# Twisted recurrence two steps at a time on GpSimd, with coefficients from VectorE and the eigenvector operations spread over the last attention halves

## What is computed

```
h = max(layernorm(x), 0);  x = x + L0(h, adj, ...)   # two graph convolutions, then LSTMs over windows of 1 to 4
h = max(layernorm(x), 0);  x = x + L1(h, adj, W, a)  # graph attention
h = max(layernorm(x), 0);  x = x + L2(h, adj, ...)   # causal attention
h = max(layernorm(x), 0);  x = x + L3(h, adj, ...)   # spectral mixer
# L3:
deg = sum(A, 0) + sum(A, 1) - diagonal(A)
L_norm = d_inv_sqrt[:, None] * (diag(deg) - A) * d_inv_sqrt[None, :]
_, U = eigh(L_norm)
out = relu((U.T @ features) @ W1 + b1) @ W2 + b2
return U @ out
```

## Time and profile before

| | us |
|---|---|
| median of 3 runs | 1045.47 |
| the 3 runs | 1045.47, 1047.27, 1044.97 |
| the profiled execution's own time | 1047.09 |
| its span (first to last instruction) | 1045.4 |
| PE busy | 873.1 |
| DVE busy | 761.5 |
| ACT busy | 493.2 |
| POOL busy | 229.3 |

### The profile page before, as it was taken

How to read it: one execution, slowest core, us unless ns; L and a number is a source line. 1 busy time by engine, 2 the same in 40 slices (tenths; PEclk the granted TensorE clock), 3 DMA queues, 4 the chain that set the end, 5 groups by cost and what they waited for, 6 DMA issues and landing times.

```text
span 1045.4 us, 14893 instructions
## 1 busy us (share of the span) xinstructions
PE 873.1 (84%) x4310; PEld 600.8 (57%) x4310; DVE 761.5 (73%) x3137; ACT 493.2 (47%) x1079; POOL 229.3 (22%) x732
## 2 busy tenths in 40 slices
PE   4689989999998999999999964999653699990598
PEld 3578865555555766766555553677442376760465
DVE  6877778887777688877777787799799696443433
ACT  0047865553434344344333310788542577860475
POOL 2111111111111111121121100121224135886000
PEclk9999999999999799999999975999976799995699
DMA  7000000000000000000000000000000000000022
GB/s 272 1 1 1 1 1 0 1 1 1 1 0 1 1 1 1 1 1 1 0 1 1 1 1 0 1 1 2 0 1 0 1 1 1 2 2 0 20 61 81
DMA packets 13976, 12.24 MB, mean 12 GB/s; under 512 B 1092, under 2 KB 10823, under 8 KB 13895
## 3 DMA queue, kind: packets, MB, share of 16 engines
q1 hardware_dynamic: 10704, 8.46, 2.5%
q10 hardware_dynamic: 3190, 2.84, 0.9%
HBM read 7.10 MB, written 4.19 MB: 11 GB/s over the span
## 4 chain that ended last, share of the span: by engine, by line
issue 49%; PE 17%; POOL 17%; DVE 15%; ACT 2%; POOLq 0%; DVEq 0%; ACTq 0%
PE bank L547 16%; POOL col_root L349 8%; POOL t L396 2%; DVE tt L785 2%; POOL PP L396 2%; DVE stat L793 2%; POOL u L396 2%; POOL XI L353 2%; DVE HT L785 1%; PE bank L557 1%; DVE X L785 1%; DVE uu L785 1%; DVE X L786 1%; POOL m L396 1%; ACT T L440 1%
## 5 line engine op out<-in xcount | busy, mean ns | idle before, releaser
L484 ACT ACTIVATE G<-bank,bias 128x512 f32<-128x512 f32 (+1 forms) x252 | 159.9, 635 | 251.7 <-PE bank L547 250.9
L547 PE MATMUL bank<-HT,wih 128*128 128x512 f32 (+1 forms) x504 | 250.6, 584 | 0.5 <-ACT HT L470 0.5
L349 POOL TENSOR_TENSOR col_root<-sa,neg_half 128x1 f32<-128x1 f32 x126 | 79.5, 631 | 491.4 <-DVE sa L787 491.4
L547 PE MATMUL bank<-H,whh 128*128 128x512 f32 (+1 forms) x288 | 136.3, 555 | 0.0
L440 ACT ACTIVATE T<-X,nbias,rstd 128x128 f32<-128x128 f32 x256 | 104.7, 487 | 39.5 <-DVE nbias L786 39.5
L444 ACT COPY T<-bank 128x512 f32<-128x512 f32 x128 | 75.0, 586 | 78.7 <-PE bank L547 50.4
L547 PEld LDWEIGHTS bank<-ST 128*128 128x128 f32 x254 | 47.9, 203 | 72.1 <-DVE ST L785 43.8
L547 PEld LDWEIGHTS bank<-HT,wih 128*128 128x128 f32 x504 | 81.0, 195 | 10.8 <-issue 4.6
L557 PE MATMUL bank<-ident,T 128*128 128x128 f32 x256 | 41.4, 287 | 43.5 <-ACT T L504 21.9
L547 PEld LDWEIGHTS bank<-XI,A 128*128 128x128 f32 x252 | 46.8, 202 | 48.8 <-DVE A L786 32.8
L547 PE MATMUL bank<-ident,ST 128*128 128x127 f32 (+62 forms) x252 | 57.5, 311 | 18.8 <-DVE ST L787 17.8
(11 more groups left out here) (331 smaller groups left out, 1855.1 us busy)
## 6 DMA issues: line engine op xcount, KB each, us to landing
out_x<-T SPq DMA_DIRECT2D x16, 256.0 KB, 2.3
wih<-in_WihT ACTq DMA_DIRECT2D x1, 1024.0 KB
whh<-in_WhhT ACTq DMA_DIRECT2D x1, 1024.0 KB
qkvT<-in_WqkvT ACTq DMA_DIRECT2D x1, 192.0 KB
wg<-in_Wg ACTq DMA_DIRECT2D x2, 64.0 KB
l3w<-in_L3W ACTq DMA_DIRECT2D x2, 64.0 KB
adjT<-in_adjT ACTq DMA_DIRECT2D x1, 64.0 KB
adj<-in_adj SPq DMA_DIRECT2D x1, 64.0 KB, 2.0
```

The costliest lines, as they stand in the source:

```text
L349: e.tensor_tensor(out=col["root"][:, :], in0=sa[:, 0:1], in1=neg_half[:, :], op=ALU.pow).then_inc(root_ready, 1)
L484: e.activation(G[x.h][:, gate, 0:n], gate_bank(k)[:, 0:n], ACT.Tanh if gate == 2 else ACT.Sigmoid, bias=bias[:, 4 * (x.p - 1) + gate:4 * ( ...
L547: mm = lambda out, l, r, start=True, stop=True: e.matmul(out, l, r, start=start, stop=stop)
```

## The change

Four parts.

1. The recurrence takes two steps at a time. From `p(s)` and `p(s-1)` both next values come as `CA * p(s) + CB * p(s-1)`, where `CA = (D0, D1*D0 + N1)` and `CB = (N0, D1*N0)` for the pair's coefficients. An operation then handles 4 elements in a partition instead of 2, and a pair of steps takes three of them (`u2`, `t2`, add). The rescaling is as before.
2. DVE computes `CA` and `CB`, in the space of the LSTM weights `wih`, behind `DLP` and `N2P`; `tw_in` is now raised four times. `N2P`'s second copy is waited for.
3. The matmul that broadcasts `lam` moves from the end of PE's attention into it, after slot 27 (`LAMBDA_AFTER`, causal attention with k = 7), and goes to bank 7.
4. The operations on the vectors are cut into parts 0 to 5. With `VECTORS` = 4, part 0 stands after half 67, part 1 after half 68, part 2 after half 69, part 3 after half 70 (`stats_1`), then `stats_2(4)`, then parts 4 and 5. The operations and their order among themselves are the same.

```diff
+VECTORS = 4
+LAMBDA_AFTER = slot_of_block(len(POINTS) * NB - 1) + 3
...
+        pair = lambda a: a.rearrange("p (s k c) -> p s k c", k=2, c=2)
+        lstm_weights = wih[:, :, :, :].rearrange("p s g o -> p (s g o)")
+        CA, CB = pair(lstm_weights[:, 0:2 * P]), pair(lstm_weights[:, 2 * P:4 * P])
...
-            e.wait_ge(tw_in, 2)
+            e.wait_ge(tw_in, 4)
             for g in range(P // KB):
-                twist(TP(u2[0][:, :], PP[:, g, 0, :], N2P[:, g * KB, :], ALU.mult))
-                for j in range(KB):
-                    s = g * KB + j
-                    k = twist.note(TP(t2[:, :], PP[:, g, j + 1, :], DLP[:, s, :], ALU.mult))
-                    if j < KB - 1:
-                        twist.note(TP(u2[(j + 1) % 2][:, :], PP[:, g, j + 1, :], N2P[:, s + 1, :], ALU.mult))
-                    e.wait_ge(ch_p, k)
-                    if s < P - 1:
-                        twist(TP(PP[:, g, j + 2, :], t2[:, :], u2[j % 2][:, :], ALU.add))
+                for j in range(0, KB, 2):
+                    n = (g * KB + j) // 2
+                    two = lambda k: PP[:, g, k, :].unsqueeze(1).to_broadcast([P, 2, 2])
+                    twist.note(TP(u2[:, :, :], two(j), CB[:, n], ALU.mult))
+                    twist(TP(t2[:, :, :], two(j + 1), CA[:, n], ALU.mult))
+                    if n < P // 2 - 1:
+                        twist(TP(PP[:, g, j + 2:j + 4, :], t2[:, :, :], u2[:, :, :], ALU.add))
...
+                if j == LAMBDA_AFTER:
+                    e.wait_ge(lam_rdy, 1)
+                    mm(bank[7][:, 0:P], bc(col["lam"][:, 0:1]), ident[:, :]).then_inc(lam_ps, 1)
...
-            e.wait_ge(lam_rdy, 1)
-            mm(bank[6][:, 0:P], bc(col["lam"][:, 0:1]), ident[:, :]).then_inc(lam_ps, 1)
...
-            e.tensor_copy(out=N2P[:, :, 0], in_=ne2p[:, 0:P]).then_inc(tw_in, 1)
-            e.tensor_copy(out=N2P[:, :, 1], in_=ne2p[:, 1:P + 1][:, ::-1]).then_inc(tw_in, 1)
+            link.note(e.tensor_copy(out=N2P[:, :, 0], in_=ne2p[:, 0:P]))
+            link(e.tensor_copy(out=N2P[:, :, 1], in_=ne2p[:, 1:P + 1][:, ::-1]))
+            by_two = lambda t: t[:, :, :].rearrange("p (s k) c -> p s k c", k=2)
+            D0, D1, N0, N1 = by_two(DLP)[:, :, 0], by_two(DLP)[:, :, 1], by_two(N2P)[:, :, 0], by_two(N2P)[:, :, 1]
+            k = link.note(TT(CA[:, :, 1], D1, D0, ALU.mult))
+            TT(CB[:, :, 1], D1, N0, ALU.mult).then_inc(tw_in, 1)
+            e.tensor_copy(out=CB[:, :, 0], in_=N0).then_inc(tw_in, 1)
+            e.tensor_copy(out=CA[:, :, 0], in_=D0).then_inc(tw_in, 1)
+            e.wait_ge(ch_e, k)
+            TT(CA[:, :, 1], CA[:, :, 1], N1, ALU.add).then_inc(tw_in, 1)
...
             while halves < N_HALVES:
                 attentions(halves)
+                vectors(halves - (N_HALVES - VECTORS))
                 halves += 1
-            e.wait_ge(tw_done, 1)
...
             stats_2(4)
...
+            for part in range(VECTORS, 6):
+                vectors(part)
```

More of the change, by code:

```diff
@@ new lines, in _, with vectors @@
+            by_half, diff2, choice, diff1 = msk[:, 16:18], msk[:, 18:20], msk[:, 20:21], msk[:, 21:22]
+            def vectors(part):
+                if part == 0:
+                    e.wait_ge(tw_done, 1)
+                    link(TS(PP[:, :, :, :], PP[:, :, :, :], 1e-26, None, ALU.add))
+                    link(e.reciprocal(out=RP[:, :, :, :], in_=PP[:, :, 1:KB + 2, :]))
+                if part == 1:
+                    link.note(TT(by_block(QQ), PP[:, :, 2:KB + 2, :], RP[:, :, 0:KB, :], ALU.mult))
+                    link(TT(by_block(RQ), PP[:, :, 1:KB + 1, :], RP[:, :, 1:KB + 1, :], ALU.mult))
+                    link(TT(gq[:, :], QQ[:, :, 0], QQ[:, ::-1, 1], ALU.add))
+                    link(TT(gq[:, :], gq[:, :], DLP[:, :, 0], ALU.subtract))
+                    link(TT(gq[:, :], gq[:, :], gq[:, :], ALU.mult))
+                    link(e.tensor_reduce(out=c("mn"), in_=gq[:, :], axis=AX.X, op=ALU.min))
+                    link(TS(msk[:, :], gq[:, :], c("mn"), None, ALU.is_le))
+                    link(STT(msk[:, :], msk[:, :], -1000.0, iota_f[:, :], ALU.mult, ALU.add))
+                    link(e.tensor_reduce(out=c("idx"), in_=msk[:, :], axis=AX.X, op=ALU.min))
+                    link(TS(c("idx"), c("idx"), 1000.0, None, ALU.add))
+                    link(TS(oneh[:, :], iota_f[:, :], c("idx"), None, ALU.is_equal))
+                if part == 2:
+                    link(TT(aB[:, :], eneg[:, 0:P], RQ[:, ::-1, 1], ALU.mult))
+                    link(TT(aF[:, :], eneg[:, 1:P + 1], RQ[:, :, 0], ALU.mult))
+                    link(e.tensor_tensor_scan(zb[:, :], aB[:, :], oneh[:, :], 0.0, ALU.mult, ALU.add))
+                    link(e.tensor_tensor_scan(zf[:, ::-1], aF[:, ::-1], oneh[:, ::-1], 0.0, ALU.mult, ALU.add))
+                if part == 3:
+                    link(TT(zb[:, :], zb[:, :], zf[:, :], ALU.add))
+                    link(TT(zb[:, :], zb[:, :], oneh[:, :], ALU.subtract))
+                    link(e.tensor_tensor_reduce(out=sq[:, :], in0=zb[:, :], in1=zb[:, :], scale=1.0, scalar=0.0, op0=ALU.mult, op1=ALU.add, accum_out=c("ss")))
+                    e.reciprocal(out=c("inr"), in_=c("ss")).then_inc(nrm_in, 1)
+                if part == 4:
+                    e.wait_ge(nrm_rt, 1)
+                    link(TS(Zn[:, :], zb[:, :], c("root"), None, ALU.mult))
+                    link(TT(sq[:, :], Zn[:, :], Zn[:, :], ALU.mult))
+                    link(e.tensor_reduce(out=en8[:, :], in_=sq[:, :].rearrange("p (a b) -> p a b", a=8), axis=AX.X, op=ALU.add))
+                    e.wait_ge(lam_ps, 1)
+                    link(e.tensor_reduce(out=c("lmax"), in_=bank[7][:, 0:P], axis=AX.X, op=ALU.max, apply_absolute_value=True))
+                    ec = ee[:, 15:127:16]
+                    link(TS(esg[:, :], ec, 0.0, 2.0, ALU.is_ge, ALU.mult))
+                    link(TS(esg[:, :], esg[:, :], 1.0, None, ALU.subtract))
+                    link(TT(pc[:, :], esg[:, :], Zn[:, 16:128:16], ALU.mult))
+                    link(TT(pc[:, :], pc[:, :], Zn[:, 15:127:16], ALU.add))
+                    link(TT(qc[:, :], pc[:, :], ec, ALU.mult))
+                    link(TS(c("lmax"), c("lmax"), 8 * 2.0 ** -24 / 2 ** .5, None, ALU.mult))
+                    link(TT(c("lmax"), c("lmax"), c("lmax"), ALU.mult))
+                    link(TT(qc[:, :], qc[:, :], qc[:, :], ALU.mult))
+                if part == 5:
+                    link(TS(qc[:, :], qc[:, :], c("lmax"), None, ALU.is_gt))
+                    link(e.tensor_reduce(out=quarters, in_=en8[:, :].rearrange("p (a b) -> p a b", a=4), axis=AX.X, op=ALU.add))
+                    link(e.tensor_reduce(out=halves2, in_=quarters.rearrange("p (a b) -> p a b", a=2), axis=AX.X, op=ALU.add))
+                    link(TT(in_first, halves2[:, 0:1], halves2[:, 1:2], ALU.is_ge))
+                    link(TT(in_first2, quarters[:, 0:4:2], quarters[:, 1:4:2], ALU.is_ge))
+                    link(TT(by_half, pc[:, 0:5:4], pc[:, 2:7:4], ALU.subtract))
+                    link(TT(by_half, by_half, in_first2, ALU.mult))
+                    link(TT(by_half, by_half, pc[:, 2:7:4], ALU.add))
+                    link(TT(diff2, pc[:, 1:6:4], by_half, ALU.subtract))
+                    link(TT(diff2, diff2, qc[:, 1:6:4], ALU.mult))
+                    link(TT(by_half, by_half, diff2, ALU.add))
+                    link(TT(choice, by_half[:, 0:1], by_half[:, 1:2], ALU.subtract))
+                    link(STT(choice, choice, in_first, by_half[:, 1:2], ALU.mult, ALU.add))
+                    link(TT(diff1, pc[:, 3:4], choice, ALU.subtract))
+                    link(STT(choice, diff1, qc[:, 3:4], choice, ALU.mult, ALU.add))
+                    link(TS(c("sign"), choice, 0.0, -2.0, ALU.is_gt, ALU.mult))
+                    link(TS(c("sign"), c("sign"), 1.0, None, ALU.add))
+                    TS(Z[:, :], Zn[:, :], c("sign"), None, ALU.mult).then_inc(z_rdy, 1)
@@ L1174, in _ @@
[L1174 to L1192, removed]
-            stats_2(4)
-            e.wait_ge(nrm_rt, 1)
-            link(TS(Zn[:, :], zb[:, :], c("root"), None, ALU.mult))
-            link(TT(sq[:, :], Zn[:, :], Zn[:, :], ALU.mult))
@@ L1201, in _ @@
[L1201 to L1229, removed]
```

17 lines of the change are left out of this document (5 added, 12 removed).

## The result

The changed kernel takes 1028.76 us (median of 4 runs: 1028.70, 1028.76, 1028.77, 1031.59), the kernel before 1045.56 us (4 runs, 1044.97 to 1047.27). The ratio is 0.9843, 95% interval 0.9823 to 0.9864. The prediction was 1028.0 us with a range of 1025.5 to 1031.0. The profiled execution took 1028.77 us with a span of 1027.0 us.

The account below looks back on a forecast made before the run. It took POOL's recurrence to bound the kernel only in DVE's last 17 us wait. Removing waits of 16.96 and 0.89 us less 0.4 us gave 17.5 us, so the median falls from 1045.47 to 1028.0, range 1025.5 to 1031.0.

Parts of the forecast that it names:

- sum: Z's transpose 17.5 us earlier (16.96 + 0.89 - 0.4); profiled execution about 1029.6 us, median 1028.0.
- Part 2: Coefficients on DVE: 1.1 us direct delay, of which PE loses 0.15 us, between 0 and 1.1.
- What bounds the kernel: POOL alone sets the end from 943 to 960 us; a faster recurrence gains at most DVE's 17 us wait.
- Part 1: POOL's recurrence: 0.70 us per pair of steps against 1.14 before, 58.0 us in all.
- upper bound of 81 us: POOL's recurrence if all three operations of each pair took 0.32 us instead of 0.20: 81.0 us.
- the backlog is gone within a period: Attention after the coefficients: DVE's up to 3.7 us waits for PE absorb the delay, leaving PE 0.15 us.
- Part 3: The lam broadcast inside PE's attention is on the path: 0.25 us, between 0.1 and 0.4.
- Part 4: DVE finds the recurrence done at 938.1, losing its 16.96 us wait; interleaving hides only 0.89 us.
- rival (c): Slower than before: interleaving costs 4.5 us behind a recurrence of 83.2 us or more; pair 1.09 us; chance 0.02.
- Rival (b): Recurrence hidden only in part: at 81.0 us the gain is 2.2 us, 1043.3; chance 0.06.
- (d): DVE stops elsewhere, at the root or nrm_rt: 1 us; chance included in the forecast's 0.80.
- The clock in L3: Same low 0.50 start of L3 after PE's gap: 0 us change, with 1.5 us either way.

Follow-up runs that it names:

- slow recurrence: Changed kernel plus one more dependent, unused 4-element POOL addition in every pair of steps; 1040.85 us median.
- spread only: Changed kernel with the old one-step recurrence and no coefficients, keeping the spread vector operations and moved lam broadcast; 1051.67 us, ratio to before 1.0042.
- two experiments that separate the parts: Changed kernel with the old one-step recurrence: 1051.67 us; changed kernel with vector operations after stats_1 and lam broadcast at attention's end: 1031.09 us.
- spare matmuls: Changed kernel plus 84 unread matmuls on PE between its attention and Z; 1026.10 us median, ratio to before 0.9804.
- the coefficients later: Changed kernel with DVE's N2P copies and coefficient operations one half later, behind att_scores(5); 1028.78 us median.
- five parts: Changed kernel with VECTORS = 5, so part 0 stands behind att_scores(15); 1026.80 us median, ratio to before 0.9810.
- all edits together: Changed kernel with VECTORS = 5, coefficients one half later, lam broadcast last and 76 unread matmuls before Z; 1021.86 us median, ratio to before 0.9769.

## Why the prediction was right

The mechanism was right, and its sum to within 1 us. The agreement of single times to 0.1 us is partly luck: a cost taken at 0.40 us measured about 1.0, and chance differences between the two profiled executions covered it (Part 2).

**What bounds the kernel.** Right. DVE's wait for POOL was nearly the whole of what a faster recurrence could give. The slow recurrence shows the limit from the other side: 18.2 us more on POOL, 10.75 us later `Z`.

**Part 1.** Right to 0.1 us: 58.1 us measured for 58.0, with the pair at 0.71 us for 0.70. The spacing of starts, not the 0.20 us durations, gave it. (The prediction's row for an operation that waits for nothing, the add at 871.85, does wait for the `t` of 871.55; the `u` and `t` at 872.48 and 872.63 of the changed kernel show the 0.15 us cleanly.) The contention that the upper bound of 81 us rested on did not occur: of the 192 operations of the pairs the slowest took 202 ns. Here the trace agrees with what was drawn from the Trainium skill (GPSIMD Engine Reference, Key points), that the contention is with VectorE instructions in a two-port mode or with two SBUF inputs. In the kernel before, four operations of the recurrence's steps stood out from the 0.20 us (0.32, 0.23, 0.23 and 0.25), all between 940.88 and 942.31, beside `stats_1`. That now runs at 947.79, after the recurrence, and the attention's multiply-adds (one input in PSUM), reductions from PSUM and `bn_stats` stretched none of the 192. No run put a two-input VectorE operation beside the new recurrence, so what it would cost there is not measured.

**Part 2.** The direct cost was right: the first attention reduction starts 1.14 us after the second `N2P` copy (872.25 - 871.11), before 0.14 us (871.04 - 870.90), so 1.0 us for the 1.1 taken. What PE loses by it was mis-sized: the term was 0.15 us, and moving the coefficients gives back 0.89, inside the bounds of 0 to 1.1 but near the upper one. The step that failed is "the backlog is gone within a period". DVE's own backlog did go (its wait in that period shrank from 2.68 to 1.66 us), but ACT's exponential hangs on the first reduction, not on DVE's average slack. In the profile of before it started 6.84 us after PE went on (871.76 - 864.92), in the changed kernel 8.60 us (872.97 - 864.37). Of these 1.76 us, 1.0 are the coefficients and 0.75 the later `lam`, and PE had not that much slack; in "spread only", with the later `lam` alone, it did not wait there.

The total agreed all the same. From `lam` to part 0's place the changed kernel took 68.08 us (938.14 - 870.06) and the one before 67.87 (937.73 - 869.86), only 0.21 more. But 0.75 us are hidden in that by the later `lam`. Counted from where PE went on, the place comes after 73.77 us (938.14 - 864.37) instead of 72.81 (937.73 - 864.92): 0.96 more, where the prediction took 0.15 + 0.25 = 0.40. This fits 0.94 for the coefficients and 0.23 for the broadcast, less 0.20 by which PE was ahead after the slow clock. That part 0 still stood at 938.14 for 938.1 is luck: PE went on at 864.37 instead of 864.92, 0.55 us earlier, a time that lies between 863.38 and 868.12 in the ten profiles.

**Part 3.** Taken at 0.25 us, read as 0.22 to 0.23.

**Part 4.** Right: part 0 found the recurrence done (at 938.14 for 938.1, with the luck just told), and the interleaving hides 0.89 us and no more. The two experiments that separate the parts measured 17.2 us for the recurrence, 0.6 for the spreading with the broadcast, and a loss of 3.7 us for the spreading with the old recurrence. The cost that rival (c) put on the spreading behind a late recurrence, 4.5 us, is real: from part 0 to the transpose it measured 4.35, of which 3.7 were left behind a recurrence that was itself 0.6 us shorter. The rival itself did not occur, as the pair cost 0.71 us, not 1.09. Rival (b) did not occur either, nor did (d): the root ran at 950.04 and `stats_2(4)` started at 950.92 without a wait.

**The clock in L3.** As forecast, L3 started at 0.50. The stretch from the transpose to the end took 67.9 instead of 68.7 us; the seven other profiles without spare matmuls show 67.5 to 68.4, the changed kernel's among them, so the one of before was on the long side. The length follows how long the granted clock stays at 0.50 from the transpose on: 8.5 us before, 7.3 in the changed kernel, 8.3 with the coefficients later (68.4 us) and 6.2 with five parts (67.5 us). What sets that time is open. This 0.8 us, inside the 1.5 us allowed, is why the profiled execution came out at 1028.77 rather than the 1029.6 of the sum. The median came out 0.8 us above the forecast because the sum carried over that the profiled execution before lay 1.6 us above its median, which the one after did not.

## What to carry to other kernels

A serial recurrence of tiny operations is priced by the spacing of starts along its dependences: merging two steps into one wider set pays nearly in full as long as the operations' duration doesn't depend on their width (0.20 us here for 2 and for 4 elements), and only until the next engine is late. Operations put between others on an in-order engine gain only the idle time of the place where they land; if what they wait for is late, everything queued behind them pays. So look for the idle stretch first and place the part in front of it (2.3 us for one constant here), and where an engine must idle before a dense stage, see what clock it will start with. A landmark inside a profile also needs a look at the clock ahead of it: here `lam` itself moved by 0.75 us against the work beside it.

## What was not expected

The time at which `lam` comes differs by 4.8 us between profiled executions whose kernels are the same up to there (869.06 to 873.81 us). A part of it lies between 120 and 160 us, in the first mixer: the same step of the reduction (the update of 128x99 elements) starts at 159.27 us in the changed kernel and at 162.08 in the one with five parts. There the granted clock was 1.00 in the changed kernel and 0.93 in the one with five parts (windows of each):

```profile
120.00:160.00 40.00, 36.37 (x245) 29.73 (x244) 30.08 (x128) 27.47 (x48) 5.60 (x17) 1.00 0.00 1
```

```profile
120.00:160.00 40.00, 36.60 (x238) 29.70 (x237) 28.57 (x125) 26.58 (x47) 5.49 (x16) 0.93 0.00 1
```

The ten profiles show 1.00, 0.96 or 0.93 in this stretch, but it isn't the whole cause: with all edits together it was 1.00, and `lam` came at 871.95. What makes the clock fall there in some executions is open. The added matmuls before L3 show the size of such things: the 7.3 us at 0.50 from the transpose on cost 2.8 us of the kernel.
